# A fused attention and expert-mixing kernel: the first check's product goes ahead of idle products, its wait is filled with statistics, and GpSimd takes over two additions and a new order of its queue

## What is computed

```python
    x = x + _layernorm(_L0_attn_ref(_layernorm(x, axis=-1), ...), axis=-1)
    x = x + _layernorm(_L0_ffn_ref(_layernorm(x, axis=-1), ...), axis=-1)
```

```python
        queries = (query @ Wq + bq).reshape(B, L, H, E)
...
        scores = jnp.einsum('blhe,bshe->bhls', queries, keys)
        A = sparsemax(scale * scores)
        out = jnp.einsum('bhls,bshd->blhd', A, values)
        out = jnp.transpose(out, (0, 2, 1, 3)).reshape(B, L, H * D)
        return out @ Wo + bo
```

## Time and profile before

| | us |
|---|---|
| median of 3 runs | 485.32 (484.76 to 485.77) |
| the profiled execution | 485.12 |
| its span, first to last instruction | 483.4 |
| PE busy | 400.4 (83%) |
| DVE busy | 313.0 (65%) |
| ACT busy | 225.9 (47%) |
| POOL busy | 149.1 (31%) |

### The profile page before, as it was taken

The page is one execution under the profiler, slowest core; times in us unless marked ns, Lnnn a source line. Parts: engine busy times, 40 slices in busy tenths (PEclk is TensorE's granted clock), DMA queues, the critical chain, the costliest instruction groups (busy, mean ns, idle before and its releaser), DMA issues. The chain is left out here.

```text
span 483.4 us, 6967 instructions
## 1 busy us (share of the span) xinstructions
PE 400.4 (83%) x2091; PEld 248.0 (51%) x2091; DVE 313.0 (65%) x1189; ACT 225.9 (47%) x412; POOL 149.1 (31%) x243
## 2 busy tenths in 40 slices
PE   3886576778897987997888998999997659999983
PEld 3543223234454554565656775734443326888872
DVE  3699999978999986675214244333332214989996
ACT  2226647646686796788434654200000001346671
POOL 3105645554858523333111110010000000335453
PEclk9997888788999998999997999999999799999998
DMA  4294011010010128458228757649999999901125
GB/s 148 86 296 131 10 44 43 1 43 27 19 43 2 62 103 298 130 182 295 90 87 301 264 176 241 255 140 392 392 395 394 393 379 356 356 5 45 55 77 174
DMA packets 44030, 83.78 MB, mean 173 GB/s; under 512 B 1878, under 2 KB 36316, under 8 KB 39388
## 3 DMA queue, kind: packets, MB, share of 16 engines
q1 hardware_dynamic: 42936, 82.15, 48.3%
q10 hardware_dynamic: 1060, 1.22, 0.8%
HBM read 70.78 MB, written 12.58 MB: 172 GB/s over the span
## 5 line engine op out<-in xcount | busy, mean ns | idle before, releaser
L1071 PE MATMUL bank<-Wz,yT 128*128 128x512 f32 x128 | 70.8, 706 | 25.9 <-DVE top L1649 23.3
L1071 PEld LDWEIGHTS bank<-Wz,yT 128*128 128x128 f32 x128 | 28.0, 228 | 61.5 <-issue 50.3
L1649 DVE MAX8 top<-bank 128x8 f32<-128x32 f32 x512 | 51.5, 180 | 1.9 <-ACT arena L746 1.7
L1007 ACT ACTIVATE d<-d 128x32 f32<-128x32 f32 x16 | 3.7, 230 | 89.4 <-DVE d L2029 89.4
L579 POOL TENSOR_SCALAR veps<-mv 128x4 f32<-128x4 f32 x24 | 5.9, 244 | 108.8 <-DVE mv L1577 76.4
L1104 PE MATMUL bank<-aWo,hoT 128*128 128x256 f32 x128 | 37.0, 413 | 0.1
L687 POOL TENSOR_TENSOR work<-work 128x512 f32<-128x512 f32 x16 | 16.6, 1058 | 64.7 <-DVE work L2104 64.7
L1138 PE MATMUL bank<-arena,Wd 128*128 128x512 f32 x64 | 29.2, 599 | 3.2 <-ACT arena L809 3.2
L1167 PE MATMUL bank<-d,work 128*128 128x256 f32 x128 | 30.6, 385 | 0.9 <-ACT d L837 0.9
L1509 PE MATMUL bank<-scr,work 128*128 128x256 f32 x128 | 29.1, 381 | 1.6 <-ACT work L1020 1.6
L1485 PE MATMUL bank<-scr,arena 128*128 128x256 f32 x128 | 28.9, 381 | 0.0
(11 more groups left out here) (267 smaller groups left out, 880.3 us busy)
## 6 DMA issues: line engine op xcount, KB each, us to landing
arena<-in_L_ffn_e_W_dram SPq DMA_DIRECT2D x10, 1024.0 KB, 7.8
x<-in_L_ffn_e_W_dram SPq DMA_DIRECT2D x9, 1024.0 KB, 9.4
arena<-in_L_ffn_e_Wg_dram SPq DMA_DIRECT2D x7, 1024.0 KB, 11.3
scr<-in_L_ffn_e_W_dram SPq DMA_DIRECT2D x7, 1024.0 KB, 13.8
work<-in_L_ffn_e_W_dram SPq DMA_DIRECT2D x5, 1024.0 KB, 14.0
xin<-in_L_attn_query_dram SPq DMA_DIRECT2D x8, 512.0 KB, 4.1
x<-in_L_attn_query_dram SPq DMA_DIRECT2D x1, 4096.0 KB, 16.5
out_dram<-x SPq DMA_DIRECT2D x8, 512.0 KB, 5.5
```

Of the source, the lines that this page charges most:

```text
L1071: mm = pe.matmul(bZ[t % 2][:, :], yT[:, c, t * P:(t + 1) * P], Wz[:, c, :], start=(c == 0), stop=(c == C - 1))
L1649: mx = v.max(top[:, h * TG + t, :], bZ[t % 2][:, h * NS:(h + 1) * NS])
```

## The change

It has three parts. In the first check PE's sum comes ahead of the idle products, of which there are 8 in the place of 10, and DVE makes `first_statistics(6)` between its comparison and the flag; the loop over groups leaves that step out. On POOL a new step `join_by_pool` adds the normed output of groups 0 and 1 to x, which `join_add` on DVE did, and `lower(i, 1)` comes ahead of `roots(2, g - 1)`. On DVE `settle(i)` comes ahead of `join_statistics(g - 1)`.

```diff
+            def join_by_pool(g):
+
+                hold(o_norm, g * TG + TG)
+                tiles = x[:, g * TG:(g + 1) * TG, :]
+                pool.tensor_tensor(tiles, tiles, o[:, g % 2, :, :], ALU.add).then_inc(x_new, 1)
+
...
             pool.wait_ge(dve_part, PREP)
+            pool.wait_ge(x_in, 16)
             values(0)
...
                     values(GB)
+                if 0 < g < GB - 1:
+                    join_by_pool(g - 1)
+                if i < NG - 1:
+                    lower(i, 1)
                 if g > 0:
                     roots(2, g - 1)
                 if i < NG - 1:
-                    lower(i, 1)
                     values(g + 1, range(2, TG))
...
             pe.wait_ge(dve_part, PREP)
-            keep_clock(7, 10)
             sum_moved(0)
+            keep_clock(7, 8)
             heads_of(0, range(3))
...
                 v.tensor_tensor(tot[:, 1, 0:n], tot[:, 1, 0:n], tot[:, 0, 0:n], ALU.not_equal).then_inc(compared, 1)
+                if b == 0:
+                    first_statistics(GB + 2)
                 hold(found, 2 * b + 1)
...
                 g = i - GB
-                if i + 2 < NG:
+                if GB < i < NG - 2:
                     first_statistics(i + 2)
                 v.wait_ge(cum, i * 3 + 3)
                 sort_top(i + 1, range(2))
                 if g > 0:
                     output_statistics(g - 1)
                 count(i, 1, False)
+                settle(i, 1, False)
                 if g > 0:
-                    join(g - 1)
-                settle(i, 1, False)
+                    join_statistics(g - 1)
```

## The result

The changed kernel takes 488.55 us in the median of 5 runs (486.59 to 489.13), the kernel before 485.32 us. The ratio is 1.0061, with a 95% interval of 1.0036 to 1.0086: about 3 us slower, where 1.6 us faster was forecast. The profiled execution took 489.13 us, the longest of the five, with a span of 487.3 us, 3.9 us more than the one before.

What follows compares the result with a forecast made beforehand. DVE was taken as nearly full from 130 to 155 us, DVE and PE to 176, PE from 192. Terms 1 and 2 together gave -1.6 us, term 3 gave 0: 485.32 - 1.6 = 483.7 us, range 482.4 to 485.1.

Steps and rivals of the forecast that it cites:

- the step: Pass i = 5: POOL's addition is not held up, as long DVE operations lie ahead of it; x new at 139.8 us.
- term 3: Pass i = 6 and after: DVE gains from the moved addition and perhaps a quicker scan, but waits for ACT and PE; 0.
- the forecast 34.65: Pass i = 5: second threshold of group 5 starts 4.2 us earlier; 34.65 us counts from the first check's comparison start.
- The addition's length: POOL's addition in pass i = 5, taken as 1.9 us from POOL's subtraction of the same size; own range 1.2 to 2.5.
- `second_norm(0)`: ACT's norm behind the second roots, now queued behind lower on POOL: to begin about 0.7 us later than before.
- the lead at `slot_scores(0)`: PE's scores behind the second norm, to come 1.6 us earlier; this is term 2, with the first check's gain in it.
- Term 1: First check: release 1.21 us earlier, DVE then waiting 1.9 us before count(4); -1.2 us, with 0 taken for PE's clock.
- The rival "slower": POOL's addition held up to 4.0 us or more uses up the lead; at 5.5 us the time is 486.8 us; chance 0.07.
- whatever holds at `slot_scores` reaches the end: From 192 us PE is full with batch 1's heads and expert-weight transfers follow it, so earlier arrival should reach the end.

Runs made afterwards that it cites:

- e9: Changed kernel plus 8 idle products in PE's gap before tile 4's product, POOL's addition also waiting for the second threshold; ratio 1.0144 to the kernel before.
- e12: Changed kernel plus 8 idle products before tile 4's product, POOL's addition cut to one column of one tile; ratio 1.0018 to the kernel before.
- e7: Changed kernel with the additions on DVE behind settle, plus 8 idle products before tile 4's product; ratio 1.0048 to the kernel before.
- e6: Whole changed kernel plus 8 idle products in PE's gap before tile 4's product; ratio 1.0072 to the kernel before.
- e11: Kernel before plus the first check's part, 8 idle products before tile 4's product and additions on POOL, in the old order; ratio 1.0018.
- e2: Changed kernel without the first check's part, which stays as in the kernel before; ratio 1.0117 to the kernel before.
- e1: Kernel before with only the first check's part (sum ahead of 8 idle products, statistics of group 6 before the flag); ratio 1.0012.
- e5: Kernel before with the first check's part and 8 idle products in PE's gap before tile 4's product; ratio 0.9976.
- e4: Changed kernel with the second roots ahead of lower again on POOL, the addition staying there; ratio 1.0083 to the kernel before.
- e8: Changed kernel with the second roots ahead of lower, plus 8 idle products before tile 4's product; ratio 1.0043 to the kernel before.

## Why the prediction was wrong

*Where the step failed.* "The long DVE operations that could hold POOL up lie ahead of the addition", and, of the hold, "only the end of `count` and `settle` run beside it, and these are short or read one tensor". I looked for a hold of POOL by long instructions of DVE. What happened is the reverse: a short instruction of DVE that begins beside POOL's addition waits for its end. Two of the five operations of `settle` were held so. A third, the last ahead of `lower`, was not beside the addition in any trace. And "short or read one tensor" was no reason: all five are short, `rcnt<-exc,rcnt` and `tauf<-tau,rcnt` read two tensors, and the held TENSOR_SCALAR reads one. The scan of 2.22 us in the earlier trace rows was the same hold, in a trace that I had: I used it for a possible gain in term 3 and not as a price here. This cost 1.4 us ahead of the threshold in the pass i = 5 and 2.1 us in the next. e9 and e12 remove it and the threshold moves to the forecast 34.65; e7 shows it the other way round.

The Trainium skill (GPSIMD Engine Reference, 8. Key points) has it that GpSimd's SBUF interfaces contend with VectorE's instructions in a 2-port mode or with two SBUF inputs. The trace agrees in kind: an instruction with two inputs in SBUF (1.67 us) and a one-input TENSOR_SCALAR in f32 (2.31 and 1.52 us) were held, and the reciprocal (0.55 us) and, in e6 and e11, the reduction beside the addition (0.69 us) were not. Not every pair of that kind is held, as the two-input row beside the power in `roots` shows (0.23 us, above). I had the rule, and weighed it only for what stood ahead of the addition.

*The addition's length* was mis-sized: 1.9 us taken, 2.35 to 2.39 measured in all seven kernels that have it on POOL. The nearest row had one operand that is repeated over 32 elements. The prediction's estimate of 2.2 us, from the Trainium skill (GPSIMD Engine Reference, 3.1 Elementwise — side-by-side cycle accounting), was nearer.

*`second_norm(0)`* was forecast at +0.7 and came at +2.66. The difference is the hold of 1.4 us and 0.5 us in the last of the roots, 0.69 us in the place of 0.20, which stood beside DVE's scan, itself an instruction with two inputs. With it the lead at `slot_scores(0)` went from -1.6 to +0.44.

*Term 3, the pass i = 6,* was put at 0 and is the larger half of the loss. `slot_scores(1)` is at +2.36, 1.92 us more than `slot_scores(0)`. Yet `second_norm(1)` is no later than `second_norm(0)` (+2.45 and +2.66). What differs is the slack behind them: from norm to scores group 0 had 8.95 us in the kernel before and needed 6.73, group 1 had 5.92 and needed 5.83. ACT waits 1.92 us for POOL ahead of `second_norm(1)`. The addition comes late (it waits for `norm_o(1)`), holds `settle` for 2.1 us, and POOL then has 3.64 us of `lower` and 2.4 of roots ahead of the norm. I had looked for what DVE would gain there and not for what POOL had to do.

*Term 1* was right on DVE (-1.33 at the release, a wait of 1.80), and wrong in its last sentence: I took 0 for PE's clock. Behind the check, after a gap of 0.81 us, the clock stayed up: `mix` of tile 0 takes 0.65 us and not 1.12. That the shorter gap is the reason is not shown. In e2 the gap there is the old 1.81 us and `mix` takes 0.65 us too. PE's products ahead of the check ran at a granted clock of 1.00 in that trace (3.67 us for eight, at 99 us), and of 0.68 in the kernel before (5.37 us, at 101 us). The first row is the kernel before, the second e2:

```profile
111.53 1.12 PE L1093 MATMUL bank<-heads 128*64 128x256 f32 x4 [0.25 <-ACT heads L777]
```

```profile
108.42 0.65 PE L1103 MATMUL bank<-heads 128*64 128x256 f32 x4 [0.25 <-ACT heads L787]
```

At the higher clock PE got further ahead, its next gap grew from 1.96 to 2.43 us (2.42 in e2), and the clock fell behind that one. By itself this takes all of the first check's gain (e1 against e5, 1.0012 and 0.9976); in the whole change it is hidden behind POOL (e6).

*The rival "slower"* had the sign right and the mechanism not: it needed an addition of 4.0 us or more that is held up on POOL, and POOL's additions took 2.36 and 2.39 us in the changed kernel.

*Right in the main:* that whatever holds at `slot_scores` reaches the end. The second release is at +2.37 and the span's end, counted alike, at +2.95, and over all traces the two go together, from e12 (-1.08 and -1.99) to e9 (+5.88 and +7.27). But the way from the release to the end took anything from 290.6 to 293.6 us, so one pair of traces cannot place 1 or 2 us there. In e4 the release is 1.33 us later than before and the end 0.18. In e5 they are 1.45 and 0.35 us earlier. The 0.6 us between +2.37 and +2.95 means nothing beside that.

*The order* costs too, and by the ratios more than the move does. e5 and e7 both have the first check's part, the idle products and the addition on DVE, and differ in the order of both lists: e7 is 2.77 us later at the second release and 0.72% slower, 3.5 us, clear of noise and on the same chip. Moving the addition in the old order (e5 to e11) costs 2.06 us at the release and 0.42%, with intervals that touch. The two do not add up: with both, e6 is 0.96% over e5. Part of e7's loss is the 0.98 us by which each `lower` is held. e12, with the new order and no addition to speak of on either engine, is 2.40 us ahead of e7 at the release and still 0.37 us behind e5, which has its addition on DVE. So most of the order's cost comes up beside an addition, whichever engine makes it. e12's timed ratio is 0.4% over e5's, with intervals that only just part, and how much of that is the order stays open.

*What stays open:* how often PE arrives at the first check with its clock down, on which the size of e5's gain depends (in the profiled executions its last scores ahead of the check took 3.67 us in four, e2, e4, e11 and e12, and 5.37 in the other ten); why the way from the second release to the end varies by 3 us; and what slows the timed runs of e2 and e4, 5.7 and 4.0 us over the kernel before, where their traces show 2.0 and 1.3 us at the second release.

## What to carry to other kernels

Before moving an elementwise operation to GpSimd, list the instructions of VectorE that will run beside it, the shortest too. Here one that reads two tensors from SBUF, and one TENSOR_SCALAR in f32, waited for its end, and what followed them waited as well. A row whose duration differs from place to place in the trace of the kernel before, as the scan's did, is the sign to look for. The move paid nothing here even where nothing else was changed (e11, 2 us worse than e5), since VectorE waited for the result. A new order of the queues around it cost as much again (e7 against e5). And where a stall is shortened, look at the next gap of PE: a gain of 1.3 us was lost to a clock that fell 24 us later, and eight idle products brought it back.

## What the runs showed of the hardware

- The exclusion goes both ways and lasts: f32 operations of 64 elements took 1.52 to 2.31 us on DVE until POOL's addition was done, and POOL's 3.64 us operation took 4.62 beside a DVE addition of 1.22 us. MAX8 from PSUM, the batch-norm statistics, reductions and the reciprocal ran at their usual length beside POOL. An operation of 64 elements that reads two tensors took its usual 0.23 us beside POOL's power on 4 elements (1.04 us).
- DVE's scan of two inputs takes 1.22 us when `lower` is over. When it starts beside `lower` it ends 1.08 to 1.09 us behind `lower`'s end, whatever that makes of its duration: 2.22 us in the kernel before, 3.62 us in e8.
- POOL adds two full tensors of 1024 f32 elements in 2.35 to 2.39 us, and takes 1.91 us when one operand is repeated.
- At one and the same place, ahead of tile 4's product, PE's granted clock fell from 1.00 to half behind gaps of 2.42 and 2.43 us (five traces), and stayed at 1.00 behind 1.96 us (one) and 0.70 us (seven). The gap alone does not settle it: at the first check, behind the same 1.81 us, it fell in the kernel before and stayed in e2.
